# Graph layer and expert network on one core: the second chunk's rows turned behind the third tile's down parts, one weight piece split behind the aggregation, x's third tile loaded by itself

## What is computed

```python
# x: 1250 x 1024, src and dst: 20000 edges, sorted by dst
h   = layernorm(x) @ W.T + b                      # eps 1e-5
deg = 1 + number of edges of each row             # self edges too
out[row] += deg[row]**-.5 * deg[col]**-.5 * h[col]   # over edges and self edges
x = x + out
flat = layernorm(x)
logits = flat @ router_w.T + router_b             # 8 experts
cw = softmax over the two largest logits
for e in range(8):                                # 1024 -> 512 -> 1024
    y = gelu(flat @ w1[e].T + b1[e]) @ w2[e].T + b2[e]
    acc += y * cw[:, e]
x = x + layernorm(acc + flat) * ln_w + ln_b       # eps 1e-12
```

## Time and profile before

| | |
|---|---|
| runs of the kernel, us | 628.86, 635.35, 629.75; median 629.75 |
| the profiled execution: its time, its span | 634.34, 632.5 |
| mean granted TensorE clock | 0.945 of full |
| PE, DVE, ACT, POOL busy, us | 540.3, 446.5, 263.7, 183.2 |
| DMA packets, MB, mean GB/s | 59277, 112.34, 178 |

### The profile page before, as it was taken

The page is one execution under the profiler, slowest core; times in us unless marked ns, Lnnn a source line. Parts: engine busy times, 40 slices in busy tenths (PEclk is TensorE's granted clock), DMA queues, the critical chain, the costliest instruction groups (busy, mean ns, idle before and its releaser), DMA issues.

```text
span 632.5 us, 12304 instructions
## 1 busy us (share of the span) xinstructions
PE 540.3 (85%) x3684; PEld 299.9 (47%) x3685; DVE 446.5 (71%) x1257; ACT 263.7 (42%) x354; POOL 183.2 (29%) x200
## 2 busy tenths in 40 slices
PE   1788999899999999997876699999999999999200
PEld 1243544455444555545652465656565655565000
DVE  8879669897065899998744748575766665655297
ACT  5333434233272343433633445454554453521470
POOL 3023000000001365652445323525253344141230
PEclk9998999899899999998997799999999999999755
DMA  6895220424327443435265967888887969173879
GB/s 235 330 371 120 40 50 15 76 57 77 57 79 287 167 162 140 168 134 195 70 192 169 276 242 185 267 208 247 230 263 213 283 189 292 35 157 89 250 208 278
DMA packets 59277, 112.34 MB, mean 178 GB/s; under 512 B 33202, under 2 KB 33615, under 8 KB 59216
## 3 DMA queue, kind: packets, MB, share of 16 engines
q1 hardware_dynamic: 49136, 80.02, 36.8%
q0 software_dynamic: 8896, 27.38, 20.7%
q10 hardware_dynamic: 1184, 4.20, 2.2%
HBM read 71.75 MB, written 33.67 MB: 167 GB/s over the span
## 4 chain that ended last, share of the span: by engine, by line
PE 74%; DVE 14%; DMA 5%; issue 4%; ACT 2%; POOL 1%; DVEq 1%; POOLq 0%; SPq 0%; ACTq 0%
PE ps L2102 7%; PE ps L2103 6%; PE ps L2104 6%; PE ps L1898 6%; PE ps L1899 6%; PE ps L2083 5%; PE ps L2084 5%; PE ps L2085 5%; PE ps L1807 4%; PE ps L1808 4%; PE ps L1809 4%; PE ps L1746 4%; PE ps L2068 4%; DVE wbufs L1324 2%; DMA wbufs<-acc_rows 1%
## 5 line engine op out<-in xcount | busy, mean ns | idle before, releaser
L2102 PE MATMUL ps<-wbufs,rows_and_counts 128*128 (+1 forms) x192 | 74.1, 386 | 6.8 <-DVE rows_and_counts L1438 3.8
L637 POOL DMA_INDIRECT acc_rows<-work,ids_out x24 | 44.3, 1845 | 114.9 <-DVE work L1499 114.6
L1493 DVE SCALAR_TENSOR_TENSOR work<-ps,wbufs 128x512 f32<-128x512 f32 x48 | 33.2, 691 | 62.4 <-PE ps L2104 62.3
L1898 PE MATMUL ps<-wbufs,rows_and_counts 128*128 128x512 f16 x200 | 75.8, 379 | 0.5 <-DVE wbufs L1324 0.5
L1899 PE MATMUL ps<-wbufs,rows_and_counts 128*128 128x512 f16 x200 | 75.8, 379 | 0.0
L2083 PE MATMUL ps<-rows_and_counts,wbufs 128*128 128x336 f16 (+1 forms) x224 | 70.2, 314 | 4.8 <-issue 4.8
L1487 DVE SCALAR_TENSOR_TENSOR wbufs<-stage,wbufs 128x1024 f16<-128x1024 f32 x56 | 67.4, 1221 | 9.6 <-ACT wbufs L970 8.5
L2103 PE MATMUL ps<-wbufs,rows_and_counts 128*128 (+1 forms) x192 | 73.9, 385 | 0.0
L2104 PE MATMUL ps<-wbufs,rows_and_counts 128*128 (+1 forms) x192 | 73.6, 383 | 0.0
L965 ACT ACTIVATE rows_and_counts<-ps 128x768 f16<-128x768 f16 x56 | 44.7, 810 | 66.6 <-PE ps L2068 63.1
L1807 PE MATMUL ps<-wbufs 128*128 128x512 f16 x160 | 63.3, 396 | 8.8 <-DVE wbufs L1131 4.0
(11 more groups left out here) (335 smaller groups left out, 1051.1 us busy)
## 6 DMA issues: line engine op xcount, KB each, us to landing
stage<-wst_in SPq DMA_DIRECT2D x72, 512.0 KB
acc_rows<-work SPq DMA_DIRECT2D x10, 512.0 KB
x_rows<-work SPq DMA_DIRECT2D x10, 512.0 KB
t<-x_in SPq DMA_DIRECT2D x1, 4096.0 KB, 13.6
wbufs<-b_in ACTq DMA_DIRECT2D x8, 512.0 KB
wbufs<-acc_rows SPq DMA_DIRECT2D x8, 512.0 KB, 7.0
t<-x_in SPq DMA_DIRECT2D x1, 3072.0 KB, 11.5
t<-x_in SPq DMA_DIRECT2D x1, 2048.0 KB, 7.8
```

What stands on the lines that cost most here:

```text
L1898: mm(o, ct_hi[:, cs], hs[:, at:at + HALF], start=(m == 0), stop=False, skip_group_check=True)
L2102: mm(down_ps[n], y_hi[:, ys], ws, start=(f == 0), stop=False)
```

## The change

On DVE, `xt_lo(1)` moves ahead of the register loads, and tile 2's statistics ahead of all one-hots; its reciprocal root stands behind window 0, its lo half behind window 1. For that x's tile 2 is loaded by a transfer of its own (`x2_in`). ACT writes tile 2's normalised rows ahead of the first count read-out, and PE does quarters 0 and 1 of tile 1's linear product ahead of window 0. SP issues the nine stores of zeros in three lots, behind the transposes of tiles 2, 3 and 4. POOL splits piece 15 behind the whole aggregation, so SP loads piece 19 behind all stores, and PE's `up_first` waits for 15 pieces, the first down part for the 16th. In the first chunk PE does down parts 3 and 4 before it turns blocks of the second chunk, and DVE makes the third tile's halves before it evicts part 3 and weighs. In `up_next` the copy for 336 rows stands first.

```diff
                if r < PIECES - 1:
                    split_lo(PIECES + r, e_hi[0], e_lo[0])
+                if r == FIRST_TILES + 1:
+                    pool.wait_ge(agg_done, 2 * NT)
+                    split_lo(2 * PIECES - 1, e_hi[0], e_lo[0])
...
-            sp.dma_start(t[:, 2 * D:].rearrange("p (r d) -> p r d", d=D),
-                         x[2 * P:, :].rearrange("(r p) d -> p r d", p=P)).then_inc(xrest_in, 16)
+            sp.dma_start(t[:, 2 * D:3 * D], x[2 * P:3 * P, :]).then_inc(x2_in, 16)
+            sp.dma_start(t[:, 3 * D:].rearrange("p (r d) -> p r d", d=D),
+                         x[3 * P:, :].rearrange("(r p) d -> p r d", p=P)).then_inc(xrest_in, 16)
...
-            sp.wait_ge(spare_in, 1)
-            for i in range(CT):
-                rows = slice(i * P, (i + 1) * P)
-                sp.dma_start(x2_rows[rows, :], zero_row).then_inc(spare_in, 16)
-                sp.dma_start(cw_rows[rows, :], zero_row[:, 0:NE]).then_inc(spare_in, 16)
-                sp.dma_start(acc_rows[rows, :], zero_row).then_inc(spare_in, 16)
             sp.dma_start(b_row[:], ln_b.partition_broadcast(P)).then_inc(lnb_in, 16)
             for m in range(BY_PE, NT):
...
+                if m < BY_PE + CT:
+                    rows = slice((m - BY_PE) * P, (m - BY_PE + 1) * P)
...
-                if r < PIECES:
+                if r < PIECES - 1:
                     piece(PIECES + STAGES + r, True)
+            piece(2 * PIECES + STAGES - 1, True)
...
+            dve.wait_ge(consts_done, EDGE_CONSTS)
+            xt_lo(1)
             extras, big = words_of(dve)
...
+            dve.wait_ge(x2_in, 16)
+            norm_stats(BY_PE)
...
+                if m == 1:
+                    norm_rstd(BY_PE)
+                    window_onehots(windows[1])
+                    xs_lo(BY_PE)
...
-                evict(0, 3, 0)
-                weights_of(0)
-                dve.wait_ge(cw_copied, 1)
-                piece_lo(0, 2, split)
-                for k in range(4):
-                    weigh_rows(0, k, 0)
                 st4.enter(0)
                 for f in range(FK):
                     dve.wait_ge(gelu_done, FK + f + 1)
                     halves_of(slice(f * CH + FIRST_CH, (f + 1) * CH), st4).then_inc(y_lo_done, 1)
+                evict(0, 3, 0)
+                weights_of(0)
+                dve.wait_ge(cw_copied, 1)
+                for k in range(4):
+                    weigh_rows(0, k, 0)
+                piece_lo(0, 2, split)
                 piece_lo(0, 3, split)
...
                 if m == 1:
                     linear(m, 0)
+                    linear(m, 1)
                     count_window(windows[0])
-                    linear(m, 1)
...
                 up_third()
-                turn4(1, 0)
-                turn4(1, 1)
-                down_part(0, 0, 3)
+                for k in range(3, 2 * CT - 1):
+                    down_part(0, 0, k)
...
-                for k in range(4, 2 * CT):
-                    turn4(1, 2 * k - 6)
-                    turn4(1, 2 * k - 5)
-                    down_part(0, 0, k)
-                turn4(1, 6)
-                turn4(1, 7)
+                for j in range(3):
+                    turn4(1, j)
+                down_part(0, 0, 2 * CT - 1)
+                for j in range(3, DK):
+                    turn4(1, j)
...
+                with pe.If(plan % 4 == 0):
+                    up(c + 1, w, BASE)
                 with pe.If(plan % 4 == 1):
                     up(c + 1, w)
-                with pe.If(plan % 4 == 0):
-                    up(c + 1, w, BASE)
```

23 lines of the change are left out of this document (15 added, 8 removed).

## The result

The changed kernel takes 627.37 us (median of 20 runs, 621.39 to 630.57), the kernel before, run beside it, 631.99 us (20 runs, 627.89 to 635.35). The ratio is 0.9939, 95% interval 0.9914 to 0.9964: 3.9 us faster, where 13.2 us were predicted. That is less than the 1% that I had called tellable from no change, but with 20 runs on each side the interval leaves no change out. Of the 10.9 us between the forecast of 616.5 and the measured 627.37, 2.2 are the base: I had the median of three runs, 629.75, and 20 runs give 631.99.

What follows compares the result with a forecast made beforehand. PE, busy 85% of the span, was taken as the bound, with gains from its waits and lower clock. Terms 4.9 + 0.9 + 7.4 = 13.2 us took the median 629.75 to 616.5 us, range 608 to 624.

Steps and rivals of the forecast that it cites:

- Front: Before window 5's end on PE: earlier tile 2 statistics and transpose gain 4.9 us: 2.8 wait, 1.7 clock, 0.4 DVE's start.
- Hand-over: At the first gathered rows: moving POOL's split of piece 15 frees DVE's add, but holds its masks; gain 0.9 us.
- First chunk: Up to the second chunk's down parts: new order starts them at 365, 9.1 us earlier, less 1.7 clock; gain 7.4 us.
- The 4.78 us before the up product I count as won: Ahead of the second chunk's up product: a 4.78 us wait without semaphore, taken as instruction fetch, vanishes with swapped branches.
- rival (e): Behind each of seven up products: jumps over unused code cost 4.78 us each; 20 us slower, 650 us; chance 0.04.
- what is won before the loops should reach the end: In the loops PE is busy 32.7 of 32.9 us at full clock, so earlier gains should last to the end.
- the chances: Whole kernel: forecast 0.45, five rivals 0.13, 0.20, 0.08, 0.10, 0.04; summed as faster 0.88, same 0.08, slower 0.04.
- no wait in the loops agrees: In the loops: the skill counts every such branch as a stall, but the trace was said to show no such wait.

Runs made afterwards that it cites:

- b_front: The kernel before with only the front's part of the change (earlier split and tile 2 statistics, own load, later zero stores): 628.13 us, ratio 0.992.
- b_swap: The kernel before with only the two branches around the up products swapped: 636.52 us, ratio 1.0053.
- b_hand: The kernel before with only weight piece 15 split behind the aggregation, and the load and waits that go with it: 631.44 us, ratio 0.9987.
- b_chunk: The kernel before with only the first chunk's new order on PE and DVE, old branches: 625.37 us, ratio 0.9861.
- a_first_only: The changed kernel with the old branch order in the loop and the second chunk's unused full-width product left out: 619.93 us, ratio 0.9817.
- h_early: a_early with half of each weight load left out from piece 20 on (weights wrong there): 617.66 us, ratio 0.9746.
- a_swap_first: The changed kernel with the 336-row branch first only for the second chunk, old order inside the loop: 624.94 us, ratio 0.9876.
- a_noswap: The changed kernel with the two branches around the up products back in their old order: 619.72 us, ratio 0.9785.
- a_early: The changed kernel with old branch order, second chunk's turned blocks and down part 5 inside both branches, so the jump comes behind down part 4: 623.88 us, ratio 0.9844.
- a_swap_loop: The changed kernel with the old branch order for the second chunk, the 336-row branch first only inside the loop: 623.16 us, ratio 0.9882.

## Why the prediction was wrong, point by point

*Front, 4.9 us: right in size, the working only in part.* PE was done with window 5 at 57.1 (I had 56.8), the split stood at 43.4 (43.5), the statistics with their sums ended at 54.5 (54.3), and b_front measures 5.0 us (3.0 to 7.0). One part was luck: 1.7 of the 4.9 was lost clock in the earlier trace rows. b_swap and b_hand, whose front is that of before, wait only 1.8 and 2.0 us at 53.8 and keep full clock, so that window 5 ends at 59.1 there, and b_front's at 58.2. Against those two profiles the front is worth under 1 us at this place, against the one that I had read 3.5.

*Hand-over, 0.9 us: not contradicted* (b_hand, 0.8, interval -0.8 to 2.5). Its steps are there: the add at 0.16 us, the masks held for 2.32 us in b_hand. In the changed kernel the masks slipped ahead of the split. Its end can't be read from the profiles: b_hand reaches the first down part at 310.41, and b_swap, which has neither front nor hand-over, at 310.46.

*First chunk, 7.4 us: right in size* (b_chunk 8.8 us, interval 6.1 to 11.4; 7.1 in its profile), *but b_chunk comes to it another way, and that is luck.* I had the up product at 342.7, the down parts at 365 because of the loads, and 1.7 us of lowered clock. In b_chunk the wait ahead of the product, which I had counted as won, grew to 6.93 us; the product starts at 349.50 and the down parts at 366.98. PE waits for no load and no halves there and keeps full clock. So the wait seems to cover what the loads would have cost; that is argued, from the next kernel. Where the wait is gone, in a_first_only, my working comes true: the down parts begin 51.6 us behind the first one against 60.7 before, 9.1 us earlier as I had it, after a wait for halves; the lowered clock takes 1.8 of that, and 7.2 are left at the end. h_early shows that the halves are late by the loads at least in part: with half the bytes the wait of 4.83 us is 2.12.

*The branches: wrong, and this is the miss.* The step that failed is "The 4.78 us before the up product I count as won", with the argument against rival (e), that in the loops the same jump costs nothing and that PE's "queue is full when the jump is read". In its place the runs showed that the same cost comes back behind the product. The queue was full, and it holds 2.7 us of work: the jump is read at 349.41 and PE runs dry at 352.11. But the jump takes 5.86 us, and behind it stand 2.2 us of register loads for the loop, which otherwise run beside the product. At the loop's copy of the code, the jump's 2.54 us would have been covered by the queue alone; the register loads behind it were not. The jump ahead of the product in the loops proved it for that place only: nothing but the product stands behind it. Even a long one is covered there: in a_swap_first it takes 2.28 us at its first pass, and PE waits 0.42. The trace of before held one price of such a jump, 4.78 us, and I booked only its removal, not its reappearance on the other side of the product.

The price is smaller than (e) had it. PE waits 5.37 us at the copy ahead of the loop, which is passed once, and 2.38 at the first pass of the loop's copy; about 2.5 and 1.8 us of lowered clock follow, then 0.3 us a loop. In all the swap costs 7.3 us of the profile, about 10 by the times. And the gain ahead of the product isn't shown to be worth anything: a_first_only, with no wait there, has a last column of 267.77, and b_chunk, with 6.93 us of wait, 267.86.

With the swap left out my sum was 13.2 us, and a_noswap measures 13.6 (11.4 to 15.8). The agreement is luck in part, since a_noswap waits 7.05 us where the sum had none. With the swap in, "what is won before the loops should reach the end" failed: 20 us of lead were 7.4 at the end. In the chances a small slip: the parts that I named add up to 0.89, 0.07 and 0.04.

The Trainium skill (Runtime: NRT & Kernel Launch, Instruction fetch mechanics) states that a taken branch out of the fetched pages stalls until the target's page is there; I had set it aside with "no wait in the loops agrees". The runs agree with it for first passes: where the jump stalls, it takes 0.9 to 6.1 us, and never at a later pass. Its other sentence, that the fetched window is two pages, would make every pass pay; behind the up products from the fourth on PE waits 0.03 us at most, and q8 moves no block between 400 and 570.

How a stop splits is shown by the traces. All kernels but a_first_only stop at their first jump over the full-width product, and in all thirteen the sequencer goes on 1.3 to 1.6 us after the block on q8 has landed; the transfer takes about 1 us. (With the old order of the branches the jump itself is short, 0.36 us, and the stop stands behind the branch that follows it.) What differs is when the block starts: 2.6 to 3.7 us behind the branch at the second up product (0.5 and 1.0 us where it is read early, in h_early and a_early), 0.2 and 0.7 us behind it at the loop's copy of the changed kernel and of b_swap, and ahead of it in a_swap_loop. Of the 2.2 us by which the wait ahead grew in b_chunk (6.93 against 4.78), 1.5 are that the sequencer is done with the branches later against PE's last work: 0.6 us before PE runs dry in the kernel before, 0.9 us after it in b_chunk.

What stays open: why a block starts so late at some jumps, and how much depends on where the code falls in the 16 KB blocks. No run moved the code without changing its order, and the stop in the middle of the third up product of a_early (2.70 us) and h_early (2.18) says that it matters.

## What to carry to other kernels

A jump over a large block of code can have a price when it is taken for the first time, and each copy of the code pays its own; a loop pays in its first pass, so a short loop pays it in a large part of its passes. Work queued ahead covers only what it lasts, and what stands behind the jump (here register loads) comes late as well. When a change removes a wait that no semaphore explains, look at the record of the branch itself, and ask where the same code is jumped to next, before counting the wait as won. And hold each gain against the next bound behind it: here the wait ahead of the up product could go or stay, and the last column was the same within 0.1 us; with the wait gone, PE waited 2.23 us for halves, and its clock fell.

## What the runs showed of the hardware

Code that was never executed cost a wait of 5.7 us by lying between two pieces that were (a_swap_first against a_first_only). A jump was dear only when it was first passed: 5.86 us for the copy ahead of the loop, 2.54 for the loop's copy at its first pass and 0.24 at its second (changed kernel). After such a stop at a first jump TensorE's sequencer went on 1.3 to 1.6 us after the block of instructions had landed, in each of thirteen kernels. The waits are as long with the DMA engines 78% busy as with 100%. And the profile's chain named a weight load as the cause of a wait that has nothing to do with it; what refuted it was a kernel in which PE went ahead before that load's piece was done.
